# A gated recurrent layer with routed experts on one core: the four mixed shared units moved ahead of the first routed one, with one-hots and weight splits over more steps

## The reference: what is computed

```
xn = layernorm(x)
s  = recurrence(xn)        # 16 heads of 8, token shift, decay per head
g  = silu(ffn(xn))
out = x + s * g
```

```
expert(t)  = (silu(t @ w1) * (t @ w3)) @ w2          # 128 -> 512 -> 128
ffn(t) = 0.5 * shared(t) + 0.5 * (p1 * expert_1(t) + p2 * expert_2(t))
```

## Time and profile before

| what | value |
|---|---|
| median of 3 runs | 740.41 us |
| the profiled execution | 740.12 us |
| its span, first to last instruction | 738.3 us |
| mean granted clock of TensorE | 0.980 |
| TensorE busy | 659.7 us (89%) |
| DVE (VectorE) busy | 572.9 us (78%) |
| ACT (ScalarE) busy | 485.2 us (66%) |
| POOL (GpSimd) busy | 456.3 us (62%) |

### The profile page before, as it was taken

The page is one execution under the profiler, slowest core; times in us unless marked ns, Lnnn a source line. Parts: engine busy times, 40 slices in busy tenths (PEclk is TensorE's granted clock), DMA queues, the critical chain, the costliest instruction groups (busy, mean ns, idle before and its releaser), DMA issues.

```text
span 738.3 us, 22304 instructions
## 1 busy us (share of the span) xinstructions
PE 659.7 (89%) x8520; PEld 458.5 (62%) x8520; DVE 572.9 (78%) x1090; ACT 485.2 (66%) x985; POOL 456.3 (62%) x493
## 2 busy tenths in 40 slices
PE   2677698997999999999999999999996899899992
PEld 1444465665665665566666667788885667676761
DVE  6989997987677886666766676676674999999992
ACT  5864578775666666566666666666665777778861
POOL 2434322225777777777777777677776566666663
PEclk9999998999999999999999999999999999999995
DMA  9931112101111333432333334333546666667730
GB/s 245 274 101 44 44 44 86 60 2 36 47 48 51 105 102 96 149 104 93 107 108 107 102 119 137 92 104 103 105 95 198 190 206 200 203 214 229 217 103 29
DMA packets 88600, 86.75 MB, mean 117 GB/s; under 512 B 11378, under 2 KB 65268, under 8 KB 88500
## 3 DMA queue, kind: packets, MB, share of 16 engines
q1 hardware_dynamic: 79412, 66.70, 28.7%
q0 software_dynamic: 9088, 18.63, 9.8%
HBM read 50.82 MB, written 34.47 MB: 116 GB/s over the span
## 4 chain that ended last, share of the span: by engine, by line
PE 46%; DVE 27%; issue 9%; POOL 8%; ACT 5%; DMA 3%; SPq 0%; POOLq 0%; DVEq 0%; ACTq 0%
PE banks L1462 7%; PE banks L1464 7%; PE banks L1463 7%; DVE hidden L1258 5%; DVE wwords L1242 5%; PE banks L1502 5%; DVE hidden L1157 4%; POOL expert_rows L612 4%; PE banks L1482 4%; PE banks L1483 4%; PE banks L1481 4%; POOL srows L602 3%; ACT hidden L730 2%; PE banks L1413 2%; DMA srows<-normed_rows,source 2%
## 5 line engine op out<-in xcount | busy, mean ns | idle before, releaser
L730 ACT CAST hidden<-hidden 128x512 f16<-128x512 f32 x206 | 127.2, 618 | 142.0 <-DVE hidden L1157 140.5
L1161 DVE TENSOR_TENSOR hidden<-hidden 128x512 f16<-128x512 f32 x178 | 122.9, 690 | 82.6 <-ACT hidden L730 81.8
L602 POOL DMA_INDIRECT srows<-normed_rows,source x142 | 148.4, 1045 | 52.6 <-issue 40.8
L1157 DVE TENSOR_TENSOR hidden<-hidden,banks 128x512 f32<-128x512 f32 x206 | 140.7, 683 | 41.5 <-ACT hidden L726 35.8
L1481 PE MATMUL banks<-wwords,hidden 128*128 (+1 forms) x824 | 149.7, 220 | 1.4 <-DVE hidden L1161 1.0
L1482 PE MATMUL banks<-wwords,hidden 128*128 (+1 forms) x824 | 149.6, 220 | 0.0
L1483 PE MATMUL banks<-wwords,hidden 128*128 (+1 forms) x824 | 149.5, 220 | 0.0
L726 ACT ACTIVATE hidden<-banks 128x512 f32<-128x512 f32 x206 | 122.7, 596 | 28.7 <-PE banks L1464 28.2
L1462 PE MATMUL banks<-sx,wwords 128*128 128x512 f16 (+1 forms) x368 | 121.5, 330 | 0.6 <-DVE sx L1150 0.6
L1464 PE MATMUL banks<-sx,wwords 128*128 128x512 f16 (+1 forms) x368 | 121.6, 330 | 0.0
L1463 PE MATMUL banks<-sx,wwords 128*128 128x512 f16 (+1 forms) x368 | 121.5, 330 | 0.0
(11 more groups left out here) (202 smaller groups left out, 1419.6 us busy)
## 6 DMA issues: line engine op xcount, KB each, us to landing
rows<-x SPq DMA_DIRECT2D x32, 256.0 KB, 5.3
rows<-expert_rows SPq DMA_DIRECT2D x32, 256.0 KB, 3.4
normed_rows<-rows SPq DMA_DIRECT2D x16, 256.0 KB, 3.9
r_rows<-rows SPq DMA_DIRECT2D x16, 256.0 KB, 2.1
rd_rows<-rows SPq DMA_DIRECT2D x16, 256.0 KB, 2.0
stage<-r_rows SPq DMA_DIRECT2D x16, 256.0 KB, 5.8
k_rows<-rows SPq DMA_DIRECT2D x16, 256.0 KB, 2.0
kd_rows<-rows SPq DMA_DIRECT2D x16, 256.0 KB, 2.1
```

The source lines that it names most:

```text
L602: G.indirect_dma_start(srows[:, q % NXB, t, :], None, rows_in, bass.IndirectOffsetOnAxis(source[:, at:at + 1], 0)).then_inc(sem[f"s_in{q % ...
L730: A.copy(guh[:, i % 4, :], gu[:, i % 2, :]).then_inc(sem["gu_hi"], 1)
L1157: V.tensor_tensor(gu[:, i % 2, :], sg[:, i % 2, :], psum[2 * (i % 2) + 1][:, :], ALU.mult).then_inc(sem["gated"], 1)
L1161: V.tensor_tensor(gul[:, i % 4, :], gu[:, i % 2, :], guh[:, i % 4, :], ALU.subtract).then_inc(sem["gu_lo"], 1)
```

## The change

`MIXED` goes from 4 to 0, so all 16 shared units stand ahead of the first routed one: `FIRST` is 16, `FIRST_STEPS` is 64, and the first routed unit begins at step 64 in place of 48. `HOT_SLOTS` goes from 28 to 44: two or three one-hot matmuls in each step in place of four or five, and `dve_source` stands in step 59 in place of 43. `SPLIT_AT` runs from 10 to 60 in place of 1 to 45. What follows from `FIRST_STEPS` follows too: POOL also has the low parts of the even steps 44 to 58. The parts of the recurrence stay at steps 75, 79 and so on. The number of steps, matmuls, gathers and scatters is the same.

```diff
-        MIXED = 4
+        MIXED = 0
         FIRST = SHARED - MIXED
...
         NHOTS = 2 * NT
-        HOT_FIRST, HOT_SLOTS, HOT_LAG = 13, 28, 3
+        HOT_FIRST, HOT_SLOTS, HOT_LAG = 13, 44, 3
...
-        SPLIT_AT = [1 + j * 44 // (3 * EXPERTS - 1) for j in range(3 * EXPERTS)]
+        SPLIT_AT = [10 + j * 50 // (3 * EXPERTS - 1) for j in range(3 * EXPERTS)]
```

## The result

The changed kernel takes 765.07 us (median of 4 runs, 763.49 to 766.29) against 740.73 for the kernel before (4 runs): ratio 1.033, 95% interval 1.029 to 1.037, so 24 us slower. The profiled execution took 764.28, with a span of 762.5. Medians in this document are over all executions, while ratios and their intervals leave out executions more than 1.5% above the fastest of their kernel.

The account below looks back on a forecast made before the run. POOL's 284 back-to-back issues were taken to bound the routed stage, DVE most of the early steps. Start +24.3 less 5.0 of waiting gives +19.3 on the profiled 740.12, so 759.4, and 759.5 us as median; range 750 to 770.

Parts of the forecast that it names:

- POOL back to back, 283 distances of 1.35 us: Routed stage: POOL's 284 gathers and scatters follow one another at 1.35 us per issue, 383 us, and bound it throughout.
- Start moves by +24.3: First gather of the routed stage: comes 24.3 us later, at about 194.4, by +32.7 - 3.0 - 5.0 - 0.4.
- Steps 0 to 12: Early stage, bound by DVE: five weight splits leave, saving 3.0 us; bounds 0 and 3.7.
- Steps 13 to 25: Early stage, bound by DVE: fewer sets, products and splits save 5.0 us; bounds 0 and 6.6.
- Steps 26 to 29: Around the gates' exponentials: the stall stays, fewer one-hots save 0.4 us; bounds 0 and 3.9.
- Steps 30 to 59: Stretch that replaces steps 30 to 43: takes 65.5 us, 32.7 more than 32.8; bounds of the increase 31.7 and 34.
- POOL wins back 5.0 us of waiting: Routed stage: of POOL's 6.7 us of real waiting for TensorE and ACT, 5.0 goes; bounds 0 and 6.7.
- The stage behind the last scatter moves as a whole: Attention stage, which waits for the scatters: shifts with the last scatter and stays as long as before.
- The rule of shared ports: DVE and GpSimd block each other: fewer DVE instructions make POOL's issues 2.8 us shorter, giving 756.7; left out of the sum.
- The early stage wins nothing: Rival: DVE's chains, not its load, hold steps 0 to 25, so both savings fail: +27.3, 768 us; chance 0.11.
- the ring of four: Rival: ACT's wait for a scatter four blocks back holds TensorE and then POOL's gathers: +25 on top, 784 us; chance 0.05.
- TensorE sets the end: Rival: POOL can issue faster when pressed, so the end follows TensorE: -7.4, 733 us; chance 0.05.

Follow-up runs that it names:

- e5: Changed kernel with one gather per block in place of two (71 of POOL's 284 issues left out): 730.93 us, ratio 0.986 to the kernel before at 741.59.
- e7: Kernel before with eight memsets on POOL between the arrival of the source list and the first gather: 746.60 us, ratio 1.0073.
- e6: Kernel before with one gather per block in place of two (the same 71 gathers left out): 737.04 us, ratio 0.995 to the kernel before at 741.59.
- e8: Kernel before with only MIXED = 0 (all sixteen shared units first, one-hots and splits not spread): 767.04 us, ratio 1.035 to the kernel before at 741.59.
- e1: Kernel before with only MIXED = 0, on a slow occasion: 845.77 us beside 840.17 for the kernel before, ratio 1.010.
- e3: Changed kernel with one gather per block in place of two, on a slow occasion: 775.89 us, 0.930 of the kernel before at 840.17.
- e4: Kernel before with one gather per block in place of two, on a slow occasion: 768.47 us, 0.921 of the kernel before at 840.17.

## Why the prediction was right

- *POOL back to back, 283 distances of 1.35 us.* Right: 389.6 / 283 = 1.377 with its waits, just above the 1.33 to 1.36 named as a sign, and 1.36 without. The rows that carried it were the count of "issue" waits and the two ends, not the busy share. e5 and e7 show it from both sides: fewer issues, and a later start.
- *Start moves by +24.3.* Measured +23.85. That it is so near was luck: four terms were off, by -2.0, +1.8, -1.7 and +1.5 us, and cancelled. Steps 0 to 12: -5.0 (forecast -3.0, beyond my bound of 3.7). Five splits are gone, as forecast, but three routing instructions also became short. Of DVE's groups there, first in the kernel before, then after:
```profile
L968 DVE SCALAR_TENSOR_TENSOR ffn<-ffn 128x512 f32<-128x512 f32 x1 | 1.6, 1645 | 0.0
L972 DVE TENSOR_TENSOR ffn<-ffn,top 128x512 f32<-128x512 f32 x1 | 1.6, 1645 | 0.0
L976 DVE TENSOR_TENSOR ffn<-ffn 128x512 f16<-128x512 f32 x1 | 1.6, 1642 | 0.0
```
```profile
L972 DVE TENSOR_TENSOR ffn<-ffn,top 128x512 f32<-128x512 f32 x1 | 0.7, 693 | 0.0
...
L968 DVE SCALAR_TENSOR_TENSOR ffn<-ffn 128x512 f32<-128x512 f32 x1 | 0.7, 691 | 0.0
L976 DVE TENSOR_TENSOR ffn<-ffn 128x512 f16<-128x512 f32 x1 | 0.7, 691 | 0.0
```
  That is 2.9 us, a term that the prediction did not have. In both kernels each of the three runs beside a low part of POOL; what changed is which of the two starts first. The first of them, before:
```profile
51.80 1.49 POOL L592 TENSOR_TENSOR hidden<-hidden 128x512 f16<-128x512 f32 x1 [0.75 <-ACT hidden L730]
52.19 1.65 DVE L968 SCALAR_TENSOR_TENSOR ffn<-ffn 128x512 f32<-128x512 f32 x1
```
  and after:
```profile
51.62 0.69 DVE L968 SCALAR_TENSOR_TENSOR ffn<-ffn 128x512 f32<-128x512 f32 x1
51.71 1.62 POOL L592 TENSOR_TENSOR hidden<-hidden 128x512 f16<-128x512 f32 x1 [0.75 <-ACT hidden L730]
```
  In the kernel before, POOL's instruction starts 0.39 us ahead in all three and DVE's takes 1.64 to 1.65; in the changed one DVE's starts 0.09 to 0.10 ahead and takes 0.69. Steps 13 to 25: -3.2 (-5.0); DVE was busy 27.6 us, as worked out, but the lumps cost 3.4 over TensorE's 27.4, not 1.6. Steps 26 to 29: -2.1 (-0.4); the granted clock was 0.86 in place of 0.77. Steps 30 to 59: 67.0 (65.5), so +34.2, just beyond my bound of 34.
- *POOL wins back 5.0 us of waiting.* The step that was mis-sized: from first gather to last scatter 0.35 us were gained and not 5.0, which is 4.65 of the 5.6 us between 759.5 and 765.07. Of 6.7 us of real waiting, 3.5 are left (nine waits, 6.2 us, minus 9 x 0.3): 3.2 won. But the issues took 301.0 us in place of 298.1, 2.9 us more, which gives nearly all of it back. I had priced an issue as a constant. The rest of the distance is the last stage (+0.7), the step from the profiled execution to the median (0.8, not 0.3), and the start (-0.45).
- *The stage behind the last scatter moves as a whole.* 762.5 - 583.58 = 178.9 against 178.2: +0.7. Right here; in e5 and e6, where POOL waits for others and ends earlier, it took 183, so the stage does not always move as a whole.
- *The rule of shared ports* (the Trainium skill, "SBUF — State Buffer", Who interferes with whom), from which I had estimated that fewer DVE instructions would make the issues 2.8 us shorter in all; it came out the other way by as much: 16 steps' DVE instructions fewer, and the issues longer. Scatters rose from 1.054 to 1.087 us, gathers fell from 1.045 to 1.033. In e7, with the same instructions as the kernel before on every engine but POOL and its issues only begun 5.9 us later, they took 301.1 us; in e8 301.9. So the number of DVE instructions alone does not set the sum. Whether the phase between the engines does, or these 3 us are what one execution differs from another by, was not isolated: each kernel has one profile at this speed.
- *Rivals.* "The early stage wins nothing" is refuted by the stretches, "the ring of four" by POOL's waits on ACT (1.8 us in all). "TensorE sets the end" was wrong for this kernel and right for e5, where TensorE is the chain in the middle.

## What to carry to other kernels

Judge an engine by the stretch in which it has work: count how many of its instructions wait for nothing, and lay its first and last against the stage. Where two engines are level, order is worth as much as work: units that one engine can do without the other are the time in which the other catches up, and bunching them ahead delays the start of the one that has no reserve. When a start moves, read what stands before it in that engine's own program, not only the semaphore it waits for.

## What the runs showed of the hardware

The same kernel took 741 us on two occasions and 839 to 840 on two others. The loss lies in the routed stage: from the first gather to the last scatter e1 took 461.7 us, and e8, the same kernel, 388.5; the time from the silu of step 0 to the first gather and the time behind the last scatter are equal within 0.3 us. In e1 the stretch 199 to 670 has a granted clock of 0.96, and TensorE's weight loads have pauses of up to 1.4 us that nothing releases, in the middle of series of matmuls (waits of the weight loads, 250 to 550):
```profile
PEld banks L1502 <- issue: 28.4, 45, 1.3
PEld banks L1481 <- issue: 15.9, 24, 1.3
PEld banks L1462 <- issue: 12.9, 28, 1.4
```
Between 250 and 550 the kernel before at 740 us has none of these. With 71 gathers fewer the pauses were shorter in sum (e3: 12.4, 9.7 and 4.0 us for L1462, L1481 and L1502), and e3 and e4 were 64 and 72 us below the kernel before. The cause stays open: none of the runs was made to tell it apart. There the change to the order alone cost 1.0% (0.4 to 1.6) in place of 3.5%; this would fit a TensorE that is shorter of time than POOL, which no run tested.
